# Projections of a two-layer decoder: values behind products, loads moved forward, stores issued by ScalarE

## The reference

```
xn  = layernorm(x) (layer 0: then rms norm);  q, k, v = xn @ W (+ b in layer 1)
layer 0: 16 heads of 16, 4 key heads, q and k times a rotation factor, causal softmax
layer 1: 16 heads of 16, scores = q.k/4 + q.rel_k[clip(j-i, -64, 64)], softmax,
         out = p.v + p.rel_v[clip(j-i, -64, 64)],  then @ W_out
```

## Time and profile before

| | us |
|---|---|
| median of 3 runs | 1770.89 (1770.38 to 1771.04) |
| profiled execution | 1768.36 |
| its span, first to last instruction | 1766.6 |
| mean granted TensorE clock | 0.945 |
| TensorE busy | 1562.5 (88%) |
| VectorE busy | 1018.2 (58%) |
| ScalarE busy | 880.8 (50%) |
| GpSimd busy | 563.4 (32%) |

### The profile page before, as it was taken

One profiled execution on the slowest core, in us unless ns is written; L12 is line 12 of the kernel. 1 busy time (PEld: TensorE's weight loads), 2 busy tenths in 40 slices (PEclk: granted clock), 3 DMA queues, 4 the chain that ended last, 5 costly groups with the idle time before them and its releaser, 6 DMA issues. The chain is left out here.

```text
span 1766.6 us, 34238 instructions
## 1 busy us (share of the span) xinstructions
PE 1562.5 (88%) x12792; PEld 1071.8 (61%) x12792; DVE 1018.2 (58%) x2084; ACT 880.8 (50%) x1468; POOL 563.4 (32%) x817
## 2 busy tenths in 40 slices
PE   7689989878479999999976799999999999996988
PEld 4233333256368767776753477777777777775544
DVE  6677777345332111111264788888888888873556
ACT  4156566632331111111134688888888888773421
POOL 3411111122313000000252455556555655542111
PEclk9799999997679999999987799999999999998999
DMA  5811111030123133221237796887868778645101
GB/s 153 237 26 29 24 24 24 2 132 22 39 75 131 63 119 128 87 86 60 61 112 153 208 222 195 203 205 200 205 200 202 210 197 200 185 137 174 49 12 36
DMA packets 209797, 213.06 MB, mean 121 GB/s; under 512 B 19652, under 2 KB 187218, under 8 KB 209506
## 3 DMA queue, kind: packets, MB, share of 16 engines
q1 hardware_dynamic: 204769, 197.24, 41.5%
q0 software_dynamic: 4864, 13.64, 2.3%
HBM read 128.82 MB, written 81.81 MB: 119 GB/s over the span
## 5 line engine op out<-in xcount | busy, mean ns | idle before, releaser
L1341 DVE CUSTOM_DVE_ANT_0 prob<-ps,dev 128x1024 f32<-128x1024 f32 x256 | 311.5, 1218 | 0.2 <-PE ps L1138 0.2
L1234 ACT ACTIVATE prob<-prob,nmax 128x1024 f32<-128x1024 f32 x256 | 293.3, 1146 | 8.3 <-DVE nmax L1341 8.3
L1158 PE MATMUL ps<-cst,prob 128*128 128x128 f32 x2048 | 279.4, 278 | 0.2
L2030 PE MATMUL ps<-xeT,w 128*128 128x384 f32 (+2 forms) x896 | 256.0, 447 | 5.1 <-DVE hT L2228 4.4
L1158 PEld LDWEIGHTS ps<-cst,prob 128*128 128x128 f32 x2048 | 228.3, 141 | 42.3 <-issue 21.0
L1370 DVE COPY probT<-ps 128x512 f32<-128x512 f32 x256 | 176.4, 689 | 104.1 <-PE ps L1158 104.0
L849 ACT ACTIVATE pT<-ps 128x512 f32<-128x512 f32 (+3 forms) x384 | 166.3, 495 | 119.3 <-PE ps L805 116.8
L887 DVE TENSOR_REDUCE nmax<-ps 128x1 f32<-128x128 f32 (+7 forms) x256 | 184.2, 753 | 69.1 <-PE ps L784 67.9
L2030 PEld LDWEIGHTS ps<-xeT,w 128*128 128x128 f32 x896 | 176.9, 198 | 77.6 <-DVE hT L2228 4.8
L2096 ACT ACTIVATE xT_c<-ps 128x256 f32<-128x256 f32 (+2 forms) x98 | 46.6, 476 | 326.0 <-PE ps L2030 325.9
L1244 ACT ACTIVATE probT<-ps 128x512 f32<-128x512 f32 x256 | 151.3, 591 | 102.4 <-PE ps L1158 102.2
(11 more groups left out here) (317 smaller groups left out, 2167.4 us busy)
## 6 DMA issues: line engine op xcount, KB each, us to landing
dev<-skew_u SPq DMA_DIRECT2D x128, 256.0 KB, 3.6
skew_p<-prob SPq DMA_DIRECT2D x128, 256.0 KB, 3.3
w<-in_L_ffn_w SPq DMA_DIRECT2D x20, 896.0 KB, 6.3
skew_u<-cst SPq DMA_DIRECT2D x64, 256.0 KB, 4.0
pre<-skew_p SPq DMA_DIRECT2D x128, 128.0 KB, 2.9
qs<-qd SPq DMA_DIRECT2D x96, 128.0 KB, 3.8
ks<-kd SPq DMA_DIRECT2D x48, 256.0 KB, 5.8
vz<-in_L_ffn_w SPq DMA_DIRECT2D x10, 896.0 KB, 5.7
```

Source lines behind the costliest of these rows:

```text
L1158: last = nc.tensor.transpose(ps[:, ring_bank(job), kb * P:(kb + 1) * P], prob_tile(t, (4 * h + kb) * P, (4 * h + kb + 1) * P), k.c("ident"))
L1234: nc.scalar.activation(prob_tile(t, 0, S), prob_tile(t, 0, S), ACT.Exp, bias=nmax[:, t % 4:t % 4 + 1], scale=-1.0).then_inc(s_exp, 1)
L1341: nc.vector.tensor_tensor_reduce(out=prob_tile(t, 0, S), in0=scores, in1=dev_tile(t), scale=-1.0, scalar=3.0e38, op0=ALU.add, op1=ALU.min, ...
L2030: last = nc.tensor.matmul(ps[:, a + z * wide + h, 0:cols], w[:, j, c, f * P:(f + 1) * P], xeT[:, c, h * cols:(h + 1) * cols], start=(c == ...
```

## The change

1. Opening: the values go behind all products on TensorE; the middle moves from GpSimd to ScalarE, one unit behind the high; the low moves from VectorE to GpSimd; the first two highs and the first middle go between the copies of the turned tiles; the two small copies go ahead on GpSimd.
2. Batch 0's projection: the pairs go q k q k by halves of the heads, so that the first six units are those of the first eight heads; the 12 loads of the first four heads (six of q behind store 8, six of k behind the last store) are issued here, into SBUF that the experts have left; all eight pairs run on TensorE before the third and fourth turn; ScalarE and VectorE take a new order.
3. Batch 1's projection: the loads are gone from its front; `front` begins with a relative product; `dev` is cleared in two parts, the first 3008 columns by VectorE, the rest by GpSimd behind the first band; the stores are issued by ScalarE, those of pair n-2 behind the highs of pair n and the middles of pair n-1, the last three at the end.

```
 Opening, TensorE
                     for i in range(3, U):
                         product(i)
-                        if i >= U - KB:
-                            value(2 * (i - U + KB))
-                            value(2 * (i - U + KB) + 1)
+                    for t in range(NT):
+                        value(t)
 Opening, ScalarE
+                    high(0)
+                    high(1)
                     turned(G - 2)
+                    middle(0)
                     turned(G - 1)
-                    for i in range(U):
-                        high(i)
-                        if i == U - 3:
-                            values(0)
+                    for i in range(2, U + 1):
+                        if i < U:
+                            high(i)
+                        middle(i - 1)
+                    values(0)
                     values(1)
 Opening, GpSimd, for each unit
                         pool.wait_ge(s_res, i + 1)
-                        nc.gpsimd.tensor_copy(parts[0:rows, i % NB, 1, :], res[0:rows, i % NB, :]).then_inc(s_mid, 1)
+                        pool.wait_ge(s_mid, i + 1)
+                        nc.gpsimd.tensor_tensor(parts[0:rows, i % NB, 2, :], res[0:rows, i % NB, :], parts[0:rows, i % NB, 1, :],
+                                                ALU.subtract).then_inc(s_lo, 1)
 Heads
-        for q in (2 * b, 2 * b + 1):
-            for c in range(DC):
+        for c in range(DC):
+            for q in (2 * b, 2 * b + 1):
 attention1
-        front = ([("project", 0), ("project", 1), ("relative", 0), ("relative", 1)] + [("project", 2), ("relative", 2)] +
-                 [("project", n) for n in range(3, 9)])
+        front = ([("relative", 0), ("project", 0), ("relative", 1), ("project", 1), ("relative", 2)] +
+                 [("project", n) for n in range(2, 9)])
 attention1, SP
-                for c in range(2 * TERMS):
-                    load(sp, 0, c, s_lq[0], s_lk[0])
-                for i in (0, 1):
-                    proj.store(sp, i)
                 band_out(0)
-                band_out(1)
                 bands_in(0)
                 bands_in(1)
-                for i in (2, 3):
-                    proj.store(sp, i)
+                band_out(1)
                 bands_in(2)
                 band_out(2)
-                for i in range(4, len(proj.units)):
-                    proj.store(sp, i)
 attention1, ScalarE, at project n
                             for i in proj.of(n - 1):
                                 proj.middle(act, i)
+                        if n > 1:
+                            for i in proj.of(n - 2):
+                                proj.store(act, i)
+                        if n == len(proj.prods):
+                            for i in proj.of(n - 1):
+                                proj.store(act, i)
 attention1, GpSimd and VectorE
-                nc.gpsimd.memset(dev[:, :], 0.0).then_inc(s_zero, 1)
                 band_of(0)
+                nc.gpsimd.memset(dev[:, THIRD:], 0.0).then_inc(s_zero, 1)
                 band_of(1)
...
+                nc.vector.memset(dev[:, 0:THIRD], 0.0).then_inc(s_zero, 1)
 experts, SP
                 for i in range(len(proj.units)):
                     proj.store(sp, i)
+                    if i == 8:
+                        proj.stored(sp, 6)
+                        for c in range(TERMS):
+                            load_part(sp, k, c, 0, q0, k0, k.s_q0, k.s_k0)
+                for c in range(TERMS, 2 * TERMS):
+                    load_part(sp, k, c, 0, q0, k0, k.s_q0, k.s_k0)
                 proj.stored(sp)
 experts, TensorE
-                for n in range(1, 6):
+                for n in range(1, KB):
                     pair(n)
                 turn(2)
-                pair(6)
-                pair(7)
                 turn(3)
 experts, ScalarE, new order of the last part
+                for n in range(5, KB):
+                    highs(n)
+                    middles(n - 1)
+                turned(2)
                 rooted(3)
                 normed(3)
+                middles(KB - 1)
                 turned(3)
 experts, VectorE, new order of the last part
+                residues(6)
+                add(KB + 7)
                 summed(3)
+                lows(5)
+                residues(7)
                 shifted(3)
+                lows(6)
+                lows(7)
```

More of the change, by code:

```diff
@@ L319, in high, with middle @@
                         nc.scalar.activation(parts[0:rows, i % NB, 0, :], f32[0:rows, i % NB, :], ACT.Copy).then_inc(s_hi, 1)
+                    def middle(i):
+                        rows = units[i][0]
+                        act.wait_ge(s_res, i + 1)
+                        nc.scalar.activation(parts[0:rows, i % NB, 1, :], res[0:rows, i % NB, :], ACT.Copy).then_inc(s_mid, 1)
                     def values(b):
@@ L409, in residue @@
                                                 ALU.subtract).then_inc(s_res, 1)
[L411 to L418, removed]
                     summed(0)
@@ L424, in _ @@
                     shifted(G - 1)
-                    for i in range(U + 2):
+                    for i in range(U + 1):
                         if i < U:
                             rotate(i)
-                        if 0 < i <= U:
+                        if i:
                             residue(i - 1)
-                        if i > 1:
-                            low(i - 2)
     FILLS = ("wa", "ctx", "wp", "g", "rel")
@@ L1239, in _ @@
                         if t == 0:
-                            for n in range(proj.deep):
-                                act.wait_ge(proj.s_st[n], 16 * ((len(proj.units) - 1 - n) // proj.deep + 1))
+                            proj.stored(act)
                         if t >= SLOTS:
@@ L1365, in _ @@
                         if t == 0:
-                            for n in range(proj.deep):
-                                dve.wait_ge(proj.s_st[n], 16 * ((len(proj.units) - 1 - n) // proj.deep + 1))
+                            proj.stored(dve)
                         if t >= SLOTS:
@@ L1846, in experts @@
     with ExitStack() as ctx:
+        with ExitStack() as over:
+            q0, k0 = k.first = first_group(k, over, "a")
+        hT = k.sb("hT", [P, FC0, ROWS], ctx=ctx)
+        xeT = k.sb("xeT", [P, DC, ROWS], ctx=ctx)
+        xe = k.sb("xe", [P, ST, D], ctx=ctx)
         wgt = k.sb("wgt", [P, B, 2, KB], ctx=ctx)
@@ L2125, in _, with highs, middles @@
                 act.wait_ge(s_bias1, 2)
[L2126 removed]
+                def highs(n):
                     for i in proj.of(n):
                         proj.high(act, i)
[L2129 to L2140 removed]
+                def middles(n):
+                    for i in proj.of(n):
+                        proj.middle(act, i)
+                highs(0)
+                turned(1)
+                for n in range(1, 4):
+                    highs(n)
+                    middles(n - 1)
+                rooted(2)
+                highs(4)
+                middles(3)
+                normed(2)
+                for n in range(5, KB):
+                    highs(n)
+                    middles(n - 1)
+                turned(2)
                 rooted(3)
                 normed(3)
+                middles(KB - 1)
                 turned(3)
@@ L2258, in _, with residues @@
                 shifted(1)
-                for n in range(KB):
+                def residues(n):
                     for i in proj.of(n):
@@ L2262, in _, with lows @@
                     proj.values(dve, n)
-                    if n:
-                        for i in proj.of(n - 1):
-                            proj.low(dve, i)
-                    if n == 4:
-                        shifted(2)
-                    add(KB + n)
-                    if n == 3:
-                        summed(2)
+                def lows(n):
+                    for i in proj.of(n):
+                        proj.low(dve, i)
+                residues(0)
+                add(KB)
+                for n in (1, 2):
+                    residues(n)
+                    add(KB + n)
+                    lows(n - 1)
+                add(KB + 3)
+                summed(2)
+                residues(3)
+                lows(2)
+                add(KB + 4)
+                shifted(2)
+                residues(4)
+                lows(3)
+                add(KB + 5)
+                residues(5)
+                add(KB + 6)
+                lows(4)
+                residues(6)
+                add(KB + 7)
                 summed(3)
-                for i in proj.of(KB - 1):
-                    proj.low(dve, i)
+                lows(5)
+                residues(7)
                 shifted(3)
+                lows(6)
+                lows(7)
 def tail_order():
```

83 lines of the change are left out of this document (38 added, 45 removed).

## The result

The changed kernel took 1759.26 us (median of 4 runs, 1756.08 to 1761.55) against 1770.64 beside it: ratio 0.9935, 95% interval 0.9918 to 0.9952, so 8.5 to 14.5 us faster. On another occasion it was 1757.70 against 1769.13, again 0.9935 (0.9921 to 0.9948). Forecast were 4.3 us, and a range that ended at 1760.5. The sign and the places were right; the size was not, and most of the miss lies in the second projection.

What follows compares the result with a forecast made beforehand. No engine fills the three touched stages; they are chains of splitting, storing and buffer reuse. Terms -3.4 + 4.4 - 5.3 = -4.3 us take the median from 1770.89 to 1766.6, range 1760.5 to 1774.5 (forecast's own 1763.5 to 1769).

Steps and rivals of the forecast that it cites:

- Opening: Before the attention: values behind the products, parts set the pace, SyncE then binds; last store at 47.4, attention at 50.7: -3.4 us.
- The contention: Opening: GpSimd's lows waiting out VectorE's residues on shared SBUF access; last two lows 1.3 us later, whole sum then -3.0.
- End of the experts: Batch 0's projection: stores 9 to 11 wait behind the moved q loads, so the next stage starts later: +4.4 us.
- the sign given: End of the experts: stores 9 to 11 land 6 us or more after issue, stage start 4 us later against the opening's shift.
- rival (a): End of the experts: stores not held up by the q loads, that stage 0, whole -8.7 us, 1762.2; chance 0.20.
- Second projection: Batch 1's projection: loads gone, ScalarE's store rounds set the end; 39.8 us to the first maximum instead of 45.1: -5.3 us.
- T: Start of the second projection, forecast at 954.1 us in the timeline.
- the walk: Second projection: estimate by rows' durations through ScalarE's store rounds, 39.8 us from the stage's start to the first maximum.
- (b): No change: opening's stores stay pushed by SyncE's loads (-1.3), one slow landing in the projection (-3.3); -0.2, 1770.7; chance 0.16.
- (c): Second projection: slower by ScalarE's own round trip, five landings in a row at 4.6 us; +4.7, 1775.6; chance 0.22.

Runs made afterwards that it cites:

- e4: The kernel before with the edits of the opening alone (values behind all products, middle casts on ScalarE, lows on GpSimd): 1765.27 us, ratio 0.9979.
- e12: The changed kernel run once more with no edit, for a reference and a second profile: 1757.70 us, ratio 0.9935 against the kernel before.
- e10: The changed kernel with the six q loads at the end of the experts behind store 6 instead of store 8: 1755.82 us, ratio 0.9929.
- e3: The changed kernel with all twelve loads at the end of the experts behind store 11, the last: 1760.76 us, ratio 0.9960.
- e2_hold: The changed kernel with ScalarE waiting before each of its stores until the middles it was just given are done: 1763.47 us, ratio 0.9970.
- e11: The changed kernel with ScalarE's stores one pair behind instead of two: 1762.83 us, ratio 0.9963.
- e1: The changed kernel with the twelve stores of the second projection issued by SyncE again, between its bands: 1759.08 us, ratio 0.9945.
- e6: The changed kernel with the twelve loads of the first heads back in front of the second projection: 1762.86 us, ratio 0.9969.

## Why the prediction was wrong, step by step

**Opening, -3.4: right in its mechanism, a little large in the profiles.** Measured -1.8 in the first profile, -2.7 in e4, -2.9 in e12. SyncE does bind as described: in e4 store 7 goes out at 40.26 (forecast 40.0), the last store at 47.48 (47.4). The rest is the 3.3 us from there to the attention, which are 3.95 in e4 and 3.7 in the changed kernel. The low on GpSimd took 1.31 us in the mean of twelve (taken were 1.2). The contention that the prediction weighed and left out of its sum is there: in the changed kernel residues that started under a running low took up to 1.64 us instead of 0.68, and lows that started under a running residue up to 1.60 instead of 1.15. But the last two lows took 1.16 and 1.15, so at the end, where it would have counted, it did not come. In the changed kernel's first profile all was a microsecond later from the first store on (26.66 against 25.58 in e4); its last store left at 48.62:

```profile
48.62 0.59 SPq L239 DMA_DIRECT2D kd<-parts  x1
...
52.36 0.27 PE L801 MATMUL ps<-ks,qs 96*128 96x128 bf16 x1 [3.80 <-PEq L204]
```

**End of the experts, +4.4: right.** Measured +4.1. VectorE's last lows began at 942.52 behind ScalarE's middles, the q loads went first, the stores waited for them and landed 6.4 to 7.7 us after their issue (the sign given was 6 or more). So rival (a) is out, though the whole time, 1759.26, lies nearer to its 1762.2 than to the forecast's 1766.6; e10, with the q loads early, comes near to what it described. What the step lacked is that SyncE's own issue, 0.56 us a load, sets the same end when the order is turned round (e3).

**Second projection, -5.3: the step that failed; measured -13.0.** Its loads, bands and clearing came as said: the split clearing is covered, band 0 is issued at 956.87 = T + 3.7 (forecast 4.4). The k loads were through earlier: the changed kernel's first band was back by T + 7.5 (960.60) where T + 11.8 was forecast. What failed is the round of ScalarE's stores, which the prediction put down as: "each round of ScalarE waits for a store that it issued itself one round before: landing 2.8 ..., hand-over 0.1, high 0.69 ..., one or two middles at 0.6, next store". The landing was rather above the 2.8 that were taken (the five store-to-high times sum to 15.8 us, where 5 x 2.9 = 14.5 were walked); the changed kernel's stores, from the line of their issue:

```profile
L618 ACTq DMA_DIRECT2D kd<-parts x8: 366/366/502, 967.3 to 984.8; - x8
...
DMA to landing us min/median/max: 2.5/3.2/4.3
```

But the length of the high in front of the store and the middles, 7.5 us in the walk, were not in the round: 0.3 us is all that lies there, because the store does not wait for the engine's work in front of it. The experiment that puts them back, e2_hold, has 7.2:

| us | forecast | changed | e2_hold |
|---|---|---|---|
| first store after T | 13.4 | 11.3 | 12.4 |
| five rounds | 22.0 | 16.1 | 22.7 |
| last of them to the first maximum | 4.4 | 4.7 | 3.5 |
| sum | 39.8 | 32.1 | 38.6 |

Of the 2.1 us at the first store, 1.1 are the same step (e2_hold has 12.4); in the rest, high 3 was through at T + 11.2, where 12.2 was walked. The bounds were missed for the same reason. The issue was bounded by 0 and 0.93 and the value 0.36 taken, SyncE's; its length is that (0.366 in the median), but it lies under a running high, so the lower bound was the price. The place of the store, behind the middles, got no bound at all. With the five rounds as they are in the changed kernel, the sum is 5.9 us lower and gives 1760.7 instead of 1766.6.

**Rivals.** (b) is out: it had -1.3 and -3.3 where -1.8 to -2.9 and -13.0 were measured. (c) is out: no landing of the changed kernel took 4.6 (most 4.3), and the issues are hidden. What did slow ScalarE as the issuer is something that no rival named: in e11, which loses 7 us of the 13, it stands 15.3 us for lows and not once for a landing. Moving the stores to ScalarE, which the prediction weighed longest, was worth some 2 us of the 13.0 (e1); about 10 to 11 come and go with the loads (e6). Against these stand the 3 to 4 us that the loads cost at the end of the experts.

## What to carry to other kernels

ScalarE's program order was not the order of its DMA issues against its arithmetic: a store whose own wait was met went out ahead of middles written in front of it that were ready, not ahead of a high whose landing was still out, and a store whose wait was not met stopped what was written behind it. So put stores on such an engine so far behind that their data are ready, and keep the engine's work in front of them off the round; in e11 one step too early cost 7 us of the 13. When loads are moved into the end of a stage, count both what queues behind them and the time the issuing queue takes for them: the stage's end waited for the one in the changed kernel and for the other in e3.

## What the runs showed of the hardware that was not expected

- In its rounds ScalarE issued its stores 0.05 to 0.1 us after the start of the high in front of them, ahead of one or two middles that stand earlier in its program; behind a high that waited 1.85 us for a landing, stores whose lows were 1.5 us old went out only once that high had started.
- Twelve loads of 128 and 256 KB held SyncE 5.8 to 6.7 us (e6, the changed kernel). The next stage began 2.4 us after SyncE's last issue where that came last (e3), 1.6 us after the last landing where that did (the changed kernel, e10).
- Sixty microseconds of the same code at a granted clock of 0.81 instead of 0.88 to 0.89 held 218 matmuls instead of 229 to 235; the last stretch of the kernel spread over 4.6 us with it, two fifths of what the change was worth. Why one execution is granted less there stays open.
